# Smaller pieces for GpSimd, and the third unit's scores earlier, in a two-layer decoder kernel

## What is computed

```python
q = rmsnorm((hidden_states @ Wq).reshape(B, Sq, H, D), gq)   # 16 heads of 128
k = rmsnorm((encoder_hidden_states @ Wk).reshape(B, Skv, H, D), gk)
v = (encoder_hidden_states @ Wv).reshape(B, Skv, H, D)
attn = softmax(einsum('bqhd,bkhd->bhqk', q, k) * scale)
x = x + einsum('bhqk,bkhd->bqhd', attn, v).reshape(B, Sq, H * D) @ Wo
```

## Time and profile before

| | us |
|---|---|
| median of three runs (2246.32 to 2248.36) | 2246.43 |
| the profiled execution, its time | 2253.14 |
| its span, from the first to the last instruction | 2251.4 |
| TensorE busy in the span | 2111.1 (94%) |
| VectorE busy | 1575.4 (70%) |
| ScalarE busy | 1258.3 (56%) |
| GpSimd busy | 564.1 (25%) |

### The profile page before, as it was taken

The page is one execution under the profiler, slowest core; times in us unless marked ns, Lnnn a source line. Parts: engine busy times, 40 slices in busy tenths (PEclk is TensorE's granted clock), DMA queues, the critical chain, the costliest instruction groups (busy, mean ns, idle before and its releaser), DMA issues. The chain is left out here.

```text
span 2251.4 us, 37700 instructions
## 1 busy us (share of the span) xinstructions
PE 2111.1 (94%) x12062; PEld 1827.8 (81%) x12062; DVE 1575.4 (70%) x3783; ACT 1258.3 (56%) x3372; POOL 564.1 (25%) x1289
## 2 busy tenths in 40 slices
PE   5999999999999899998899999999999998589993
PEld 5899999999898678887788888888888887378882
DVE  6777777777778884434667667666766677767776
ACT  5554555445455533324666666666666666467772
POOL 1000000001001122223333334333333433144541
PEclk9999999999999999999999999999999999789997
DMA  6121112111210220002111111111111111278886
GB/s 239 65 90 71 65 51 79 47 70 49 76 65 20 71 75 1 1 1 75 47 57 48 57 62 59 47 56 47 56 47 57 73 39 38 85 258 287 293 280 256
DMA packets 75394, 194.77 MB, mean 87 GB/s; under 512 B 8432, under 2 KB 39176, under 8 KB 63008
## 3 DMA queue, kind: packets, MB, share of 16 engines
q1 hardware_dynamic: 65440, 172.55, 22.0%
q0 software_dynamic: 7680, 16.80, 2.2%
q10 hardware_dynamic: 2176, 4.19, 0.5%
HBM read 176.73 MB, written 25.17 MB: 90 GB/s over the span
## 5 line engine op out<-in xcount | busy, mean ns | idle before, releaser
L653 PE MATMUL bank<-l_wkv_hi,l_ctxT 128*128 128x256 f32 (+1 forms) x1024 | 277.5, 343 | 9.7 <-PEq L78 7.1
L1074 DVE TENSOR_TENSOR l_pT_lo<-bank,l_pT_hi 128x512 fp32r<-128x512 f32 x256 | 175.1, 684 | 76.7 <-ACT l_pT_hi L916 76.0
L1074 DVE TENSOR_TENSOR l_v_lo<-bank,l_v_hi 128x128 fp32r<-128x128 f32 (+1 forms) x256 | 91.6, 358 | 184.6 <-ACT l_v_hi L891 183.2
L910 ACT ACTIVATE l_probs<-l_scored,l_nbias 128x256 f32<-128x256 f32 x256 | 128.2, 502 | 158.9 <-DVE l_nbias L1127 155.7
L653 PE MATMUL bank<-xnT_hi,l_wq_hi 128*128 128x512 f32 x512 | 209.7, 410 | 0.0
L653 PE MATMUL bank<-l_wo_hi,l_oT_hi 128*128 128x512 f32 x512 | 208.6, 407 | 0.7 <-DVE l_oT_lo L1074 0.7
L653 PEld LDWEIGHTS bank<-l_wkv_hi,l_ctxT 128*128 128x128 f32 x1024 | 181.9, 191 | 33.2 <-issue 8.1
L653 PE MATMUL bank<-xnT_lo,l_wq_hi 128*128 128x512 f32 x512 | 201.4, 393 | 0.0
L653 PE MATMUL bank<-xnT_hi,l_wq_lo 128*128 128x512 f32 x512 | 201.2, 393 | 0.0
L653 PE MATMUL bank<-l_wo_hi,l_oT_lo 128*128 128x512 f32 x512 | 200.5, 392 | 0.0
L653 PE MATMUL bank<-l_wo_lo,l_oT_hi 128*128 128x512 f32 x512 | 200.2, 391 | 0.0
(11 more groups left out here) (287 smaller groups left out, 5913.4 us busy)
## 6 DMA issues: line engine op xcount, KB each, us to landing
l_ctxT<-ctx_split SPq DMA_DIRECT2D x63, 1024.0 KB, 4.8
moe_raw_gu<-in_L_ffn_gate_up_proj SPq DMA_DIRECT2D x32, 1024.0 KB, 6.9
moe_raw_dn<-in_L_ffn_down_proj SPq DMA_DIRECT2D x32, 512.0 KB, 5.5
l_raw_a<-in_L_xattn_Wq SPq DMA_DIRECT2D x16, 512.0 KB, 5.8
l_raw_a<-in_L_xattn_Wo SPq DMA_DIRECT2D x16, 512.0 KB, 5.5
x_sb<-in_x SPq DMA_DIRECT2D x4, 1024.0 KB, 8.7
moe_raw_gu<-moe_y_rows SPq DMA_DIRECT2D x4, 1024.0 KB, 11.8
out_x<-x_sb ACTq DMA_DIRECT2D x8, 512.0 KB, 9.5
```

The costliest lines, as they stand in the source:

```text
L653: mm = nc.tensor.matmul(out, a[x], b[y], start=(i == 0), stop=(i == n - 1))
L910: ins = nc.scalar.activation(probs[u % 2][:, t, :], src, ACT.Exp, bias=nbias[:, i:i + 1], scale=scale, accum_out=rsum[:, i:i + 1])
L1074: nc.vector.tensor_tensor(pair[1], src, pair[0].bitcast(F32), ALU.subtract).then_inc(done, 1)
```

## The change

Three edits. GpSimd's low parts of the weights are computed in pieces of 256 columns (PIECE), and so is the scaling of the keys; the semaphore is signalled by the last piece. In the second attention, scores(2) move from behind turn_p(1) to ahead of sum_q(0) of the next group. TensorE no longer waits for q_ready; VectorE waits for it in `biases` of the units 0 and 2.

```diff
     def weights_lo(pool, w, raw, level, done):
         pool.wait_ge(a.w_hi, level)
-        nc.gpsimd.tensor_tensor(w[1], raw, w[0].bitcast(F32), ALU.subtract).then_inc(done, 1)
+        across = w[1].shape[1:]
+        step = max(1, across[0] * PIECE // math.prod(across))
+        for i in range(0, across[0], step):
+            at = slice(i, i + step)
+            ins = nc.gpsimd.tensor_tensor(w[1][:, at], raw[:, at], w[0][:, at].bitcast(F32), ALU.subtract)
+        ins.then_inc(done, 1)
...
-                gp.tensor_tensor(kn3, kn3, scale, ALU.mult).then_inc(k_ready, 1)
+                for i in range(0, nk, PIECE // HD):
+                    at = slice(i, i + PIECE // HD)
+                    ins = gp.tensor_tensor(kn3[:, at, :], kn3[:, at, :], scale[:, at, :], ALU.mult)
+                ins.then_inc(k_ready, 1)
...
                 if b == 0:
                     pe.wait_ge(q_split, count(HB, h + 1, hg, g))
-                    if rms:
-                        pe.wait_ge(q_ready, count(HB, h + 1, hg, g))
...
+                    scores(hg, g, 2)
                     if rms:
                         sum_q(hg, g + 1, 0)
-                    else:
-                        scores(hg, g, 2)
-                    if rms:
                         weigh_v(hg, g, 0)
                     project_kv(hg, g, 2)
                     project_kv(hg, g, 3)
                     if not rms:
                         weigh_v(hg, g, 0)
                     turn_p(hg, g, 1)
-                    if rms:
-                        scores(hg, g, 2)
-                    elif ending(hg, g):
+                    if not rms and ending(hg, g):
                         turn_late(0, 1)
...
                 dve.wait_ge(s_made, count(UN, u + 1, hg, g))
+                if rms and u % 2 == 0:
+                    dve.wait_ge(q_ready, count(HB, u // 2 + 1, hg, g))
```

More of the change, by code:

```diff
@@ L42 @@
 EPS = 1e-5
+PIECE = 256
 SM_SCALE = float(HD) ** -0.5
```

## The result

The changed kernel took **2255.86 us** (median of 14 runs, 2252.12 to 2257.54), the kernel before 2249.93 us beside it (14 runs, 2246.32 to 2254.05). The ratio is **1.0024**, with a 95% interval of 1.0016 to 1.0032: slower by 0.24%, which is 5.4 us; the two medians are 5.9 us apart. The forecast was 2257.2 us. The profiled execution took 2256.23 us with a span of 2254.5 us, 3.1 us more than the profiled one of before on both counts; I work the accounts out against that pair.

A forecast was written before the change was run, and what follows sets the result against it. TensorE was taken to bound the second attention's groups. Debts of 28.2 us (29 groups at 0.95, plus 0.4 and 0.2) minus gains of 17.4 gave +10.8 us on the median of 2246.43: 2257.2 us, range 2240 to 2265.

The forecast's parts named there:

- The gains: Second attention: TensorE's stalls per head pair, 1.75 us around wo_lo and 0.48 us at a weight cast, vanish; 17.4 us.
- The debt of the order: Second attention: scores(2) moved ahead make project_kv(3) 0.71 us later, so TensorE is 0.57 us late at turn_p(3) per group.
- The pieces of kn: GpSimd's key scaling in four pieces of 256 columns takes 2.29 us, 0.39 more than whole.
- Probs(3): On VectorE, ahead of turn_p(3): held back by the key scaling's fourth piece, losing 0.38 us, bounds 0 and 0.55.
- The debt in all: Second attention: TensorE is 0.57 + 0.38 = 0.95 us late at turn_p(3) in 29 groups, 27.6 us.
- The first attention: TensorE's order stays and VectorE's waits on GpSimd have cover, so the pieces there were costed at nothing.
- The moved wait: On VectorE, the wait for q_ready never holds; the second semaphore on its reduce costs nothing to 0.08 us.
- D: GpSimd's queued pieces never let go of the port, so nbias(1) waits for all four; 2268.6 us, chance 0.08.
- B: Pieces let VectorE through, probs(3) lose nothing, only the reordering's 0.57 us a group remains; 2246.1 us, chance 0.27.
- C: The chain from project_kv(3) to probs(3) has slack, so only the holes are filled; 2229.6 us, chance 0.15.

The follow-up runs named there:

- early maxima: Changed kernel with the key scaling whole, and VectorE's biases(2) of the second attention moved ahead of split_kv(2): 2241.98 us, ratio 0.9959 to the kernel before.
- early maxima and keys in pieces: Changed kernel, key scaling still in pieces, with VectorE's biases(2) of the second attention moved ahead of split_kv(2): 2234.93 us, ratio 0.9926 to the kernel before.

## Why the prediction was right, and where not

**The direction and the mechanism were right.** Gains in two places of a pair, a debt in every group, the debt made of two waits for normalised probabilities: the profile shows just these. Step by step:

- The gains. The 1.75 and the 0.48 us are both gone, since all groups are equal. But the prediction never asked what each edit wins alone: the pieces alone win 1.53 of the 1.75, and the order adds 0.22 + 0.48 us per pair, about 5 us in all, for a debt of 0.42 to 0.44 us in 29 groups, some 12.5 us. Whole keys in the new order against the old one: 2242.57 to 2235.69, 6.9 us slower.
- The debt of the order: sized at 0.57 us, measured at 0.42 (order alone) to 0.44 (whole keys, 26.24 to 25.80). The term that failed is the time from VectorE's end to TensorE's start. I took 0.15 us from the one row where weigh_v waits for pT_lo. At turn_p it is 0.05 to 0.06: probs(2) end at 1296.71 and the transposes start at 1296.77, probs(3) at 1301.06 and 1301.11. With 0.05 the spare time at turn_p(3) is 0.24 instead of 0.14, and 0.71 - 0.24 is 0.47. The lower bound that I gave for it, 0.50 from a release in 0.08 us, was still too high. What is left between 0.47 and the measured 0.42 to 0.44 is the other place: with whole keys TensorE waits at turn_p(2) alone, where 0.34 - 0.05 = 0.29 us were spare and 0.71 - 0.29 = 0.42 are not, and turn_p(3) begins 0.07 to 0.09 us after probs(3) end.
- The pieces of kn: 2.29 us predicted, 2.33 measured (625 ns a piece, 0.61 predicted). Probs(3): 0.38 us longer predicted, 1.01 to 0.62 measured, 0.39. The group grows by just this, from 26.24 to 26.63. This was the most precise step, because the earlier trace rows held a row in which the same hold showed at the same place.
- The debt in all: 0.95 predicted, 26.63 - 25.80 = 0.83 measured. 29 times the 0.12 us are 3.5 us too many.
- The second attention: 29 x 0.83 = 24.1, plus 0.4, minus 17.4, is +7.1; the trace shows +6.8.
- The first attention: "VectorE's waits on GpSimd there have cover, and I cost the pieces in it at nothing" was wrong by 3.7 us. I had gone by TensorE's waits, which from 100 to 700 us of the kernel before are this one row (total us, times, longest):

```profile
PE bank L653 <- DVE l_pT_lo L1074: 1.1, 6, 0.2
```

The lengths of the groups would have shown what it stood for: every fourth was 22.25 to 22.29 us, in the same pattern as the earlier trace rows, which I had made for the second attention only. The wait of 0.18 us is counted from the recorded end of the matmul ahead, 175.27 + 0.28 = 175.55. Where nothing waits the next one starts 0.12 us after the start before, so weigh_v is 0.34 us late, and the matmuls behind it, the second of which follows 0.20 us after the first, add 0.12 more.
- The moved wait held nobody in the changed kernel, as said: no wait of VectorE for q_ready is listed, and the edit alone measures 1.0002. With the early maxima it does hold VectorE.

The two sizes that were off, 3.5 us of debt and 3.7 us of gain, both made the forecast too high against the profiled pair (+10.8 against +3.1). The runs side by side give +5.9 us between medians, and their kernel before is itself at 2249.93, 3.5 us above the median that I started from; so the nearness of 2257.2 to 2255.86 is partly luck: the forecast change of +10.8 us was 4.9 too high even beside these +5.9, and the higher median of the kernel before took back 3.5 of that.

**The rivals.** D fell: nbias(1) took 0.28 us with three pieces queued behind the first. B fell with probs(3) at 1.01 us, though its price, 0.57 us a group for the order, was also too high. C fell, since there is a wait in every group. But C was right in one half: the pieces without the order and without the keys are its 'only the holes are filled', 2235.69 us.

On the rule of the Trainium skill, "SBUF — State Buffer", section "Who interferes with whom", that the one that issues first has the shared pair for its whole instruction: the trace agrees with the instruction as the unit of the lock, since VectorE came in after one piece of four. It doesn't agree with a lock to GpSimd's recorded end, which by the prediction's working would have held probs(3) for 0.55 us and made the pair 1.17 us, where 1.01 was measured.

**What kn in pieces costs in the old order.** It is 0.2 us a group (26.0 against 25.78) though 0.39 minus the spare 0.24 is only 0.15. The two parts can be read: turn_p(3) begins 0.14 us later behind turn_p(2) (4.05 us in place of 3.90), and turn_k another 0.06 us later behind turn_p(3), the price of the late start.

**What stays open.** With early maxima and keys in pieces the groups are 0.34 to 0.47 us above 25.75, and the hold of probs(3), 1.17 - 0.62 = 0.55 us less the spare 0.40, accounts for 0.15 of them; no run separates the rest. Nor does one show why weigh_v starts 0.14 us behind its release and a transpose 0.05. And whether the key scaling can be placed where VectorE doesn't meet it was not tried.

## What to carry to other kernels

Cut an operation that holds another engine back where that engine asks early in it, and leave it whole where the other asks near its end: the cut lengthens the hold by the fixed part of each piece, and the same cut cost 0.39 us a group in one place and gave 0.2 in another. Moving work ahead on the bounding engine makes all that follows late by its length, so look first at the spare time of each of its waits; a fix that works off the critical engine should be timed without the reordering that comes with it: here the pieces of the weights alone were the faster kernel, 0.9935. And cut every stage in windows of its period, since a short wait of 0.18 us was a 0.46 us loss, 14 us after its cause.

## What the runs showed of the hardware

- TensorE's transposes of probabilities start 0.05 to 0.06 us after the VectorE instruction that they wait for (1296.71 to 1296.77, 1301.06 to 1301.11; with whole keys 0.05). Weigh_v after pT_lo takes 0.14 to 0.15 (1317.60 to 1317.74 with the order alone, and the earlier trace rows). The price of a release is read for each pair of instructions. Four transposes that start so close behind it take 0.66 us, and 0.60 where they had spare time.
- Between GpSimd's queued pieces VectorE gets its turn: 0.28 us for nbias(1) in the changed kernel, 0.27 with the weights alone, against 1.94 beside the whole operation. The pieces then end later: kn takes 2.43 us where the pair meets it early, 2.33 where late.
- The fixed part of a GpSimd operation, some 0.18 us by an estimate from these rows, is only a little hidden by the piece ahead of it: 128 columns of the key scaling take 0.40 us, 256 take 0.625, 1024 take 1.90, and four pieces of 256 together 2.33, which is 0.43 more for three more fixed parts.
- A tensor_scalar of VectorE with one tensor input is held by GpSimd as well: nbias of the first attention, 128x2, took 1.83 us beside the whole wo_lo, asked 0.58 us after its start, and 0.18 us when asked 0.59 us after the start of a first piece of 0.74; probs of 128x256 took 0.62, 1.01, 1.17 or 1.52 us a pair, according to where in kn they asked.
